# Placing each use of the spare PSUM bank whole behind the step's attention values, and four uses of the output projection instead of two

## The reference

```python
q_t, k_t, v_t = (split_heads(layernorm(x) @ W.T) for W in (W_q, W_k, W_v))
q_h, k_h, v_h = exp_map(q_t), exp_map(k_t), exp_map(v_t)     # tanh of the row's norm times its direction
arg = max(1 + 2c * |q_h - k_h|^2 / ((1 - c|q_h|^2) * (1 - c|k_h|^2)), 1 + EPS)
weights = softmax(-beta * arccosh(arg) / sqrt(c) - attention_bias)
x = x + concat(log_map(exp_map(weights @ log_map(v_h)))) @ W_o.T
xq = fp8_e4m3fn(bf16(layernorm(x)) / s_in);  kq = fp8_e4m3fn(kernel / s_k)
x = x + bf16((xq @ kq) * s_in * s_k) + bias
```

## Time and profile before

| | us |
|---|---|
| median of 3 runs | 1992.58 (1991.73 to 1993.07) |
| the profiled execution | 1994.49 |
| its span, first to last instruction | 1992.7 |
| ScalarE busy | 1869.9 (94%) |
| TensorE busy | 1788.6 (90%) |
| VectorE busy | 1142.9 (57%) |
| mean granted clock of TensorE | 0.972 |
| first exponential starts, last ends | 57.2, 1955.9 |

### The profile page before, as it was taken

The page is one execution under the profiler, slowest core; times in us unless marked ns, Lnnn a source line. Parts: engine busy times, 40 slices in busy tenths (PEclk is TensorE's granted clock), DMA queues, the critical chain, the costliest instruction groups (busy, mean ns, idle before and its releaser), DMA issues.

```text
span 1992.7 us, 29554 instructions
## 1 busy us (share of the span) xinstructions
PE 1788.6 (90%) x10713; PEld 603.1 (30%) x10713; DVE 1142.9 (57%) x2825; ACT 1869.9 (94%) x1094; POOL 12.8 (1%) x35
## 2 busy tenths in 40 slices
PE   7988989989898798989998898998989899899897
PEld 4322222323232232322322223232322223233234
DVE  7454565655656656565656647565565656323436
ACT  4889999999999799999998999999999999999883
POOL 2000000000000000000000000000000000000000
PEclk9799999999999899999999899999999999999889
DMA  1314213141312213132040321314131131411110
GB/s 56 112 49 144 54 54 103 42 134 43 112 44 78 77 44 112 43 101 75 23 134 22 110 67 44 112 43 134 40 107 52 56 90 43 123 43 53 33 33 23
DMA packets 112953, 142.54 MB, mean 72 GB/s; under 512 B 35691, under 2 KB 61548, under 8 KB 112748
## 3 DMA queue, kind: packets, MB, share of 16 engines
q1 hardware_dynamic: 112748, 140.13, 22.6%
HBM read 85.07 MB, written 55.05 MB: 70 GB/s over the span
## 4 chain that ended last, share of the span: by engine, by line
ACT 54%; PE 24%; issue 14%; DVE 4%; ACTq 3%; DMA 0%; DVEq 0%; SPq 0%
ACT U L1217 28%; ACT U L1224 26%; PE ps L1100 8%; PE ps L401 6%; PE ps L1115 5%; ACTq L1265 2%; PE ps L695 2%; DVE U L1294 1%; PE ps L1138 1%; PE ps L406 1%; PE ps L1142 1%; DVE U L1285 1%; DVE rows L554 0%; DMA U<-in_L_attn_W_o_dram 0%; ACT e L529 0%
## 5 line engine op out<-in xcount | busy, mean ns | idle before, releaser
L1224 ACT ACTIVATE U<-U 128x2048 f32<-128x2048 f32 x512 | 997.1, 1949 | 0.3
L1217 ACT ACTIVATE U<-ps 128x2048 f32<-128x2048 f32 x500 | 955.7, 1911 | 35.5 <-PE ps L1100 31.6
L1100 PE MATMUL ps<-q_T,k_T 18*128 18x512 f32 x4096 | 632.5, 652 | 133.0 <-ACT U L1217 107.7
L1115 PE MATMUL ps<-U,vals 128*32 128x512 f32 x4096 | 560.4, 620 | 29.4 <-ACT U L1224 28.9
L1100 PEld LDWEIGHTS ps<-q_T,k_T 18*128 18x128 f32 x4096 | 195.9, 187 | 356.8 <-ACT U L1217 296.4
L401 PE MATMUL ps<-wT,xnT 128*128 128x384 f32 x512 | 232.0, 545 | 4.9 <-DVEq L1318 2.5
L490 DVE COPY qkv<-ps 128x384 f32<-128x384 f32 x112 | 62.4, 557 | 243.7 <-PE ps L401 243.6
L1115 PEld LDWEIGHTS ps<-U,vals 128*32 128x32 f32 x4096 | 81.7, 109 | 205.4 <-ACT U L1224 159.2
L401 PEld LDWEIGHTS ps<-wT,xnT 128*128 128x128 f32 x512 | 81.1, 194 | 197.0 <-issue 132.4
L1138 PE MATMUL ps<-woT,ident 128*128 128x256 f32 x340 | 121.8, 441 | 3.8 <-DVEq L1318 3.6
L406 PE MATMUL ps<-ident,rows 128*128 128x128 f32 x512 | 107.2, 308 | 4.9 <-DVE rows L554 2.4
(11 more groups left out here) (209 smaller groups left out, 1179.6 us busy)
## 6 DMA issues: line engine op xcount, KB each, us to landing
rqb<-q_scratch SPq DMA_DIRECT2D x64, 1024.0 KB, 5.6
q_scratch<-q_T SPq DMA_DIRECT2D x16, 1024.0 KB, 4.5
k_scratch<-k_T SPq DMA_DIRECT2D x16, 1024.0 KB, 6.8
v_scratch<-vals SPq DMA_DIRECT2D x16, 768.0 KB, 9.6
fi_xt<-in_L_attn_x_dram SPq DMA_DIRECT2D x17, 512.0 KB, 6.0
xt<-in_L_attn_x_dram SPq DMA_DIRECT2D x15, 512.0 KB, 6.7
out_dram<-fi_x SPq DMA_DIRECT2D x15, 512.0 KB, 4.6
rk_scratch<-rk SPq DMA_DIRECT2D x16, 32.0 KB, 12.5
```

The lines of the kernel that those rows point to most:

```text
L1100: ins = pe.matmul(g.ps[:, 2 * pair + i, :], a.k_T[HB * h:HB * h + RD, b % 2, hg, kt * P:(kt + 1) * P], a.q_T[HB * h:HB * h + RD, G % 3, hg ...
L1115: ins = pe.matmul(g.ps[HB * h:HB * h + VW, 6, :], a.vals[:, b % 2, kt, (hg * HPG + h) // 2, DH * (h % 2):DH * (h % 2) + VW], U[:, n % RING ...
L1217: act.activation(U[:, n % RING].rearrange("p b n -> p (b n)"), chunk(n), ACT.Ln, scale=-2.0 / EPS, bias=1.0).then_inc(freed, 1)
L1224: act.activation(U[:, n % RING], U[:, n % RING], ACT.Exp, scale=exponent).then_inc(exp_done, 1)
```

## The change

Every use in PROJECT_USES and FINISH_USES moves to position 1, whole behind V, but Y 0. The W uses become four of one tile each. Slots are dealt out anew for most uses and for VectorE's pieces; the calls of tile 0's and tile 1's stores and of ScalarE's small exponential (scalar, slot 21 to 22) follow. R uses of the queries now come before those of the keys in what they wait for. SECOND_USES keeps some uses half and half. SHORT_SLOTS starts to gather slots at step 10 instead of 23, SHORT_USES goes, and BARE becomes step 5.

```diff
-PROJECT_SLOTS = 35
-FINISH_SLOTS = 34
-PROJECT_USES = {("X", 0): (4, BOTH), ("X", 1): (5, BOTH),
-                ("M", 0): (7, BOTH), ("M", 1): (8, BOTH), ("M", 2): (9, BOTH), ("M", 3): (10, BOTH),
-                ("M", 4): (12, BOTH), ("M", 5): (13, BOTH), ("M", 6): (15, BOTH), ("M", 7): (16, BOTH),
-                ("R", 0): (25, BOTH), ("R", 1): (26, BOTH), ("R", 2): (27, 0), ("A", 0): (27, 1),
-                ("R", 3): (28, BOTH), ("R", 4): (29, BOTH), ("R", 5): (31, 0), ("A", 1): (31, 1),
-                ("R", 6): (32, BOTH), ("R", 7): (33, BOTH)}
+PROJECT_SLOTS = 37
+FINISH_SLOTS = 35
+PROJECT_USES = {("X", 0): (4, 1), ("X", 1): (5, 1),
+                ("M", 0): (7, 1), ("M", 1): (8, 1), ("M", 2): (10, 1), ("M", 3): (11, 1),
+                ("M", 4): (12, 1), ("M", 5): (15, 1), ("M", 6): (16, 1), ("M", 7): (17, 1),
+                ("R", 0): (26, 1), ("R", 1): (27, 1), ("R", 2): (28, 1), ("A", 0): (28, 1),
+                ("R", 3): (29, 1), ("R", 4): (30, 1), ("R", 5): (31, 1), ("A", 1): (31, 1),
+                ("R", 6): (32, 1), ("R", 7): (33, 1)}
-FINISH_USES = {("T", 0): (13, BOTH), ("T", 1): (14, BOTH), ("W", 0): (15, BOTH), ("W", 1): (17, BOTH),
-               ("Q", 0): (30, BOTH), ("Y", 0): (31, 0), ("Y", 1): (31, 1)}
-
-SHORT_USES = dict(FINISH_USES)
-SHORT_USES.update({("Q", 0): (28, BOTH), ("Y", 0): (30, 0), ("Y", 1): (30, 1)})
-BARE = 7
-SHORT_SLOTS = {23: (23, 24), 24: (25, 26), 25: (27, 28), 26: (29,), 27: (30, 31), 28: (32,), 29: (33,), 30: (), 31: ()}
+FINISH_USES = {("T", 0): (9, 1), ("T", 1): (14, 1), ("W", 0): (15, 1), ("W", 1): (16, 1),
+               ("W", 2): (17, 1), ("W", 3): (19, 1),
+               ("Q", 0): (30, 1), ("Y", 0): (31, 0), ("Y", 1): (31, 1)}
+BARE = (5,)
+
+SHORT_SLOTS = {10: (10, 11, 12, 13), 11: (14,), 12: (15,), 13: (16,), 14: (17, 18), 15: (19,), 16: (20, 21), 17: (22,),
+               18: (23,), 19: (24,), 20: (25,), 21: (26, 27), 22: (28, 29, 30), 23: (31, 32), 24: (33,), 25: (34,),
+               26: (), 27: (), 28: (), 29: (), 30: (), 31: ()}
...
 FIRST_USES = {("A", 0): (2, 0), ("R", 4): (2, 0), ("A", 1): (2, 0), ("R", 5): (3, BOTH), ("R", 6): (6, BOTH),
-              ("R", 7): (11, BOTH), ("R", 0): (14, BOTH), ("R", 1): (17, BOTH), ("R", 2): (19, BOTH),
-              ("R", 3): (20, BOTH)}
+              ("R", 7): (14, BOTH), ("R", 0): (17, BOTH), ("R", 1): (19, BOTH), ("R", 2): (20, BOTH),
+              ("R", 3): (21, BOTH)}
...
-SECOND_USES.update({("R", 0): (25, BOTH), ("R", 1): (26, BOTH), ("R", 2): (27, 0), ("A", 0): (27, 1), ("R", 3): (28, 0),
-                    ("R", 4): (28, 1), ("R", 5): (29, BOTH), ("R", 6): (30, 0), ("A", 1): (30, 1), ("R", 7): (31, BOTH)})
+SECOND_USES.update({("M", 2): (9, BOTH), ("M", 4): (12, BOTH), ("M", 5): (13, BOTH), ("M", 6): (15, BOTH), ("M", 7): (16, BOTH),
+                    ("R", 0): (26, 1), ("R", 1): (27, 0), ("A", 0): (27, 1), ("R", 2): (28, 0), ("R", 3): (28, 1),
+                    ("R", 4): (29, BOTH), ("R", 5): (30, 0), ("A", 1): (30, 1), ("R", 6): (31, 0), ("R", 7): (31, 1)})
...
-    OWN = {0: 9, 1: 10, 9: 2, 11: 2, 14: 2, 17: 3, 18: 4, 19: 6, 20: 2, 21: 6, 22: 5, 23: 4}
+    OWN = {0: 9, 1: 10, 9: 2, 12: 2, 16: 2, 18: 3, 19: 4, 20: 3, 21: 3, 23: 6, 24: 5, 25: 4}
...
-    OWN = {3: 1, 4: 2, 6: 11, 21: 9, 22: 10, 23: 4, 24: 2, 25: 2, 28: 2, 32: 1}
+    OWN = {3: 1, 4: 2, 6: 11, 15: 1, 16: 1, 17: 1, 19: 1, 20: 5, 22: 10, 23: 4, 24: 2, 25: 2, 27: 2, 33: 1}
...
         elif kind == "W":
-            for a in halves(part, range(2)):
-                t = 2 * i + a
-                for dc in range(2):
-                    ins = pe.matmul(bank[:, a * D:(a + 1) * D], ocT[:, dc, t * P:(t + 1) * P],
-                                    g.woT[:, dc, :], start=dc == 0, stop=dc == 1)
+            for dc in halves(part, range(2)):
+                ins = pe.matmul(bank[:, 0:D], ocT[:, dc, i * P:(i + 1) * P], g.woT[:, dc, :],
+                                start=dc == 0, stop=dc == 1)
...
-            v.tensor_tensor(x1[:, two, :].rearrange("p t d -> p (t d)"),
-                            xt[:, two, :].rearrange("p t d -> p (t d)"), bank, ALU.add).then_inc(b7_copied, 1)
+            v.tensor_tensor(x1[:, i, :], xt[:, i, :], bank[:, 0:D], ALU.add).then_inc(b7_copied, 1)
...
-        if k == 21:
-            v.wait_ge(b7_copied, uses.after(("W", n, 1)))
-            for t in range(GT):
-                step.mark(v.bn_stats(stats[:, t, :], x1[:, t, :]))
+        if k in (15, 16, 17, 19):
+            t = {15: 0, 16: 1, 17: 2, 19: 3}[k]
+            v.wait_ge(b7_copied, uses.after(("W", n, t)))
+            step.mark(v.bn_stats(stats[:, t, :], x1[:, t, :]))
+        if k == 20:
```

More of the change, by code:

```diff
@@ L366, in sync @@
             sp.dma_start(xt[:, :, :], g.x_g[n + 1]).then_inc(x_in, 16)
-        if k == 34:
+        if k == 36:
             b, u = n // 2, n % 2
@@ L426, in tensor @@
             if kind == "R" and i % HG == 0:
-                pe.wait_ge(rows_rdy, 2 * n + 2 - i // HG)
+                pe.wait_ge(rows_rdy, 2 * n + (1 + i // HG if n >= 2 else 2 - i // HG))
         ins = fill(pe, n, key, g.ps[:, 7, :], part)
@@ L526, in scalar @@
     def scalar(act, n, k):
-        if k == 21:
+        if k == 22:
             act.wait_ge(n_rdy, n + 1)
@@ L538, in first_vector @@
         step(v.tensor_scalar(ss[:, :, :], ss[:, :, :], EPS * EPS, None, ALU.max))
[L539 to L545, removed]
+        for k in (19, 20, 21, 35):
+            if k == 35 and n == 0:
+                v.wait_ge(zeroed, ZEROED)
+            vector(v, n, k, step)
+        vector(v, n, 23, step)
+        vector(v, n, 24, step)
         if n == 1:
             v.wait_ge(p_filled, len(FIRST_FILLS))
-        vector(v, n, 23, step)
+        vector(v, n, 25, step)
         scale_rows(v, n, (1, 0) if n == 0 else (1,))
@@ L582, in vector @@
             ins.then_inc(xn_rdy, 1)
-        if k in (9, 11, 14, 17):
-            t = {9: 0, 11: 1, 14: 2, 17: 3}[k]
+        if k in (9, 12, 16, 18):
+            t = {9: 0, 12: 1, 16: 2, 18: 3}[k]
             v.wait_ge(a.b7_copied, uses.after(("M", n, 2 * t + 1)))
@@ L590, in vector @@
                 step(v.tensor_scalar(ss[:, :, :], ss[:, :, :], EPS * EPS, None, ALU.max))
-        if k == 18:
+        if k == 19:
             root_guess(v, step, ss[:, :, :], y[:, :, :])
             newton(v, step, ss[:, :, :], y[:, :, :], y2[:, :, :], 1)
-        if k == 19:
-            newton(v, step, ss[:, :, :], y[:, :, :], y2[:, :, :], 2)
+        if k == 20:
+            newton(v, step, ss[:, :, :], y[:, :, :], y2[:, :, :], 1)
+        if k == 21:
+            newton(v, step, ss[:, :, :], y[:, :, :], y2[:, :, :], 1)
             v.tensor_tensor(nrm[:, :, :], ssqk, yqk, ALU.mult).then_inc(n_rdy, 1)
-        if k == 20:
+        if k == (31 if n == 2 else 35):
+            step = first or Steps(v, g_steps, 2 * (n - 2))
             step(v.tensor_scalar(vg[:, :, :], y[:, :, 2 * H:], g.ZS, 1.0, ALU.mult, ALU.min))
@@ L607, in vector @@
                                 ALU.mult).then_inc(v_rdy, 1)
-        if k == 21:
+        if k == 23:
             v.wait_ge(e_rdy, n + 1)
@@ L621, in vector @@
             step(v.reciprocal(rp[:, :, :], a4[:, :, :]))
-        if k == 23:
+        if k == 25:
             if n >= 4:
@@ L629, in vector @@
             v.tensor_reduce(amax[:, :], a4[:, :, :].rearrange("p t h -> p h t"), AX.X, ALU.max).then_inc(amax_rdy, 1)
-        if k == 24:
-            scale_rows(v, n, (1, 0))
-        assert first or step.n == OWN.get(k, 0), (k, step.n)
+            if n >= 2:
+                scale_rows(v, n, (0,))
+        if k == 26:
+            scale_rows(v, n, (1,))
+        assert first or k in (31, 35) or step.n == OWN.get(k, 0), (k, step.n)
     p = Shared()
@@ L670, in sync @@
             if n >= 1:
-                sp.wait_ge(steps_v, PER * (n - 1) + sum(count for slot, count in OWN.items() if slot <= 28))
+                sp.wait_ge(steps_v, PER * (n - 1) + sum(count for slot, count in OWN.items() if slot <= 27))
             sp.dma_start(xt[:, :, :], g.x_g[n]).then_inc(f_in, 16)
-        if k == 33:
+        if k == 34:
             sp.wait_ge(res_rdy, n + 1)
@@ L962, in in_step @@
                     found.append(("S", x // HG, x % HG))
-            found += [(kind, n, i) for n, k in finished(G, s) for kind, i in at(finish_uses(n), k, half)]
+            found += [(kind, n, i) for n, k in finished(G, s) for kind, i in at(FINISH_USES, k, half)]
             found += [(kind, n, i) for n, k in projected(G, s) for kind, i in at(project_uses(n), k, half)]
@@ L982, in finished @@
             return [(n, k) for n, k in slots if 0 <= k < FINISH_SLOTS]
-        def finish_uses(n):
-            return SHORT_USES if n == LAST - 1 else FINISH_USES
         uses = Uses()
@@ L1054, in _ @@
                 project.first_sync(sp, 2)
-                project.sync(sp, 0, 34)
+                project.sync(sp, 0, 36)
                 load_rq(0)
@@ L1061, in _ @@
                     if n == 21:
```

(8 more changed lines are left out.)

18 lines of the change are left out of this document (9 added, 9 removed).

## The result

| | before | after |
|---|---|---|
| median | 1992.15 us (1986.07 to 1993.07, 6 runs) | 2098.41 us (2088.41 to 2103.72, 6 runs) |
| the profiled execution, its span | 1994.5, 1992.7 | 2095.5, 2093.7 |
| mean granted clock | 0.972 | 0.936 |

The change makes the kernel slower: the ratio is 1.0534, 95% interval 1.0503 to 1.0566, or 106 us. The forecast was 2040 in a range of 1990 to 2100. The number landed on that of rival C, at the end of the range.

What follows compares the result with a forecast made beforehand. ScalarE, busy 94%, was taken to set the pace, so TensorE's order matters through when D arrives. Late D's +26, waits removed -17 and clock falls +39 gave +48 on a median of 1992.6: 2040 us, range 1990 to 2100.

Steps and rivals of the forecast that it cites:

- rival C: TensorE's clock falls in half of the places: +105 us, 2098 us; chance 0.13.
- late D's: Distances from TensorE reach ScalarE late after M, R and A move: 2.0 us per group, +26 us in 13 groups.
- falls of the clock: TensorE's clock drops at newly opened holes: 13 falls at 3 us each, +39 us.
- open units: VectorE's pieces in the two open units besides group 15's stay about the same in sum: 0 +- 3 us.
- what goes: Waits removed in groups 0, 14 and 15 and step 26, less group 15's added VectorE work: -17 us.
- the 65: Five places per group, steps 3, 11, 19, 27 and after the bare step, where clock falls were expected: 13 falls.
- the one seen: The clock fall behind bare step 7 of group 15 in the kernel before: ScalarE lost 3.7 us.
- every second M is late: In neighbouring steps every second whole M delays D by 0.32 us: five per group, 1.6 us.
- step 24: R 2 with A 0 behind V, waiting for VectorE to empty bank 7: over the budget by 0.6 us.
- steps 26 and 27: R 4 in the step of the sums late by 0.5 us, A 1 in the step behind by 0.2.
- Rival B: A whole M behind V is no longer late, so the kernel gets faster: 1964 us, or 1981; chance 0.17.
- Rival A: TensorE's clock holds and only the late D's remain: +9 us, 2001 us; chance 0.14.

Runs made afterwards that it cites:

- run 2: The changed kernel with VectorE's last Newton pass and nrm one slot earlier (slot 20 instead of 21): 2069.99 us, ratio 1.0396 to the kernel before.
- run 1: The changed kernel with a pair of unread matmuls between D and V in steps 3, 5, 11, 19 and 27: 2059.13 us, ratio 1.0352 to before.
- run 3: The changed kernel with both unread matmul pairs in steps 3, 5, 11, 19, 27 and nrm one slot earlier: 2028.09 us, ratio 1.0194 to before.
- run 4: The changed kernel with the eight M uses half and half again, in their new slots: 2066.30 us, ratio 1.0398 to the kernel before.
- run 6: The kernel before without the unread matmuls of steps 19 and 20: 1998.20 us, ratio 1.0043 to the kernel before.
- run 9: The changed kernel with nrm early and W 3 between D and V of step 19: 2048.10 us, ratio 1.029 to the kernel before.
- run 5: The kernel before with M whole behind V in its old slots, from group 1 on: 2007.16 us, ratio 1.0091 to the kernel before.
- run 11: The kernel before with selected parts: group 0's M 3 and R 1, four W uses, step 7 bare only in groups 1-13, Q, tile 1's last uses: 1971.14 us.

## Why the prediction was wrong

In the terms of its sum, forecast and found (from the profiled executions):

| term | forecast | found | from |
|---|---|---|---|
| late D's, 13 groups | +26 | +26 | group 6: 118.27 - 115.14 = 3.13, less 1.16 for e, x 13 |
| e waits for nrm | 0 | +15 | interval at step 18, run 2 |
| falls of the clock | +39 | +66 | the rest of 114.2; 35 falls at 1.9 us |
| open units, groups 5 and 8 | 0 +- 3 | +7 | 1.9 and 5.3 |
| what goes | -17 | -13 | group 0, 14, 15, prologue, tail |
| sum | +48 | +101 | |

- **The step that failed is the size of the clock term:** "I take one fall in five places, 13, at 3 us each". It measured 66 us: 35 falls outside the open units at 1.9 us. The mechanism and the sign held; runs 1, 3, 4, 6 and 9 show it by filling or making the holes. The places held in part. Of the 65, 25 had one of these falls: step 4 (9), 12 (5), 19 or 20 (10), one at 7, and none behind a hole of step 27. The other ten falls, at steps 26 and 27, came behind the waits for VectorE (A 0, the emptying of bank 6, R 4), which the prediction named ("plus the waits of A and R 4") but gave no falls. Those at 19 and 20 stood behind a hole of 1.97 us that it had not foreseen. Each cost less than the one seen: 1.65 us at steps 4 and 12, about 1.4 at 26 and 27, 1.5 to 3.9 at 19 and 20. In the trace of before one place of two had a fall, and I had weighed that as one in five.
- **A wait was missed.** The prediction left e at "0.3, which stays", and named no wait for its move from slot 21 to 22. It adds 1.16 us per group, and it lengthens the hole behind it; run 2 gives 28 us for both between the medians.
- **Open units.** "About the same in sum" compared VectorE's work, not when its inputs come. The copy of W 3 stood whole behind V in the step just ahead of group 8's unit, in part under a fallen clock; run 9 takes back 4.5 us by its position alone.
- **What goes** was 4 us too high: group 0 is 6.2 shorter by its own length (with the prologue 8.5), not 9.4. Group 15 won 8.5 us at its bare step and at the wait of Q (7.7 forecast), but gave 5.9 back in the intervals of steps 11 to 16, around its open unit, where 1.3 was expected. Both forecasts took a wait of the one trace of before as its fixed price. In run 6 the same code of group 0 took 130.70 us, 1.0 less than in after, and in run 5 that of group 15 took 118.50, 3.7 less than in after: what the change wins in these groups is not settled by one execution of each.
- **What held.** A whole M takes 1.49 us to the next instruction (forecast 1.51); every second M is late, at 0.25 to 0.31 (0.32); step 24 is late by 0.4 to 0.6 (0.6); steps 26 and 27 together 0.9 (0.5 + 0.2); the steps of W are free at 3.56. Rival B is out: 1.17 us pass from the start of D to the logarithm behind a whole M (837.63 to 838.80), as with half ones in the earlier trace rows. Rival A falls with the clock, 0.936.
- Rival C's number, 2098, is that of the measurement, and its count, 32, is close to the 35 found; but ten of these stand outside its 65 places, and at 1.9 us instead of 3 they make 66 of its 96. The rest came from e and the open units. Its agreement in the time is partly luck.

What stays open: why the clock holds at the same pair of holes in some groups and not in others (run 5 against after). Falls repeat at the same step in groups of like length, and shift when a length changes; more than that the runs don't show.

With e's wait and most of the falls taken out (run 3), the profiled execution's span is 30 us over that of before: 32 us of late D's, of which 7.5 are the added pair of step 27, about 11 of falls, 5 of the open units, less 17 in group 0, 14, 15, the prologue and the tail. That closes the account to within 1 us. (The medians are 36 apart; the profiled execution of before is its slowest here, that of run 3 its fastest.)

## What to carry to other kernels

Work in front of a wait that is there anyway is free twice: it hides, and it keeps TensorE busy enough that the clock holds; moved behind, it costs what goes over the room there and leaves a hole. So before such a move, list the places where nothing is left between two waits, and price each with the share of such places that already fail in the trace; two places are few for that, and one traced execution too. When a table of slots is dealt out anew, follow each small instruction on the bounding engine (here e, 0.4 us) to its producer's new place, and ask of each piece what stands behind it when it comes: a few parts of this change, most of them moving a use off a wait for VectorE, gave 18 us when taken alone (run 11).

## What the runs showed of the hardware

- An idle of 0.70 us before a D and one of 0.56 before the next V, in a queue that is otherwise nearly full, were enough for TensorE's clock to go from 2.4 to 1.2 GHz, in 15 of 37 such places outside the open units. With 0.70 us of unread matmuls in the second of these idles the granted clock of the same 7 us was 1.00 instead of 0.76, and none of these 15 falls is left (run 1).
- The Trainium skill ("TensorE: Matmul & The Clock Gate") has both rules, as the prediction said. These traces agree with its section "A second HAM failure mode: psum-queue depth-cycling", that frequent short idles do it, and not with "HAM oscillation", by which it takes a long one: in the 8 us before any of the 35 falls no idle is longer than 1.97 us.
- Matmuls that nobody reads, added to TensorE, made a program 39 us faster that another engine bounds.
- The price of a fall is what stands in it: 1.65 us where a whole M does (steps 4 and 12 of after), 1.2 to 1.5 where short uses do (run 6), up to 3.9 behind the hole of 1.97 us (steps 19 and 20 of after).
